# Attention and expert stages of a spiking layer with routed experts: two steps of the expert weights' split set a block apart, scatters ahead of attention, first expert rows loaded inside it, sums moved to GpSimd

## The reference, cut to what matters

```python
xn = layernorm(x)                                   # x: 2 x 2048 x 256, float32
x + attn(xn) + ffn(xn)

# attn, D = 256, 16 heads of 16
Q, K, V = [spike(layer_norm(xn @ W.T + b, g, beta) - 1) for each of q, k, v]    # 0 or 1
attn = Dh - (q_sum + k_sum - 2 Q K^T) + log_pe_bias                            # no softmax
out = spike(attn * scale @ V - 0.5)
out = spike(layer_norm(out @ Wo.T + bo, go, betao) - 1)

# ffn, E = 8 experts, top 2
scores, idx = top_k(softmax(xn @ router_w.T), 2); scores /= sum(scores)
out = sum over the two experts of score * (silu(xn @ up[:, :256]) * (xn @ up[:, 256:])) @ down
```

## Time and profile before

| what | us |
| --- | --- |
| median of 3 runs (lowest to highest) | 446.23 (444.5 to 446.79) |
| the profiled execution's own time | 447.23 |
| its span, first to last instruction | 445.4 |
| TensorE busy in it | 369.1 (83%) |
| VectorE, ScalarE, GpSimd busy | 272.4, 226.1, 231.5 |
| mean granted TensorE clock | 0.951 of full |

### The profile page before, as it was taken

The page is one execution under the profiler, slowest core; times in us unless marked ns, Lnnn a source line. Parts: engine busy times, 40 slices in busy tenths (PEclk is TensorE's granted clock), DMA queues, the critical chain, the costliest instruction groups (busy, mean ns, idle before and its releaser), DMA issues.

```text
span 445.4 us, 9584 instructions
## 1 busy us (share of the span) xinstructions
PE 369.1 (83%) x2421; PEld 297.8 (67%) x2430; DVE 272.4 (61%) x899; ACT 226.1 (51%) x716; POOL 231.5 (52%) x203
## 2 busy tenths in 40 slices
PE   4399848899888987666945999999999999999980
PEld 1233738888888554444744888888888888888760
DVE  5699799987877425555735455555555555555530
ACT  1456773777876543333422455555555555555530
POOL 3646424777773025543713455547374656554663
PEclk9589896999999999999979899999999999999995
DMA  8842031344544025655454455646475566564653
GB/s 262 283 166 72 0 93 51 121 133 154 173 140 147 1 60 167 192 189 165 146 164 143 66 96 96 104 83 107 82 113 93 100 97 101 93 105 85 104 60 35
DMA packets 43399, 51.71 MB, mean 116 GB/s; under 512 B 6278, under 2 KB 37000, under 8 KB 43368
## 3 DMA queue, kind: packets, MB, share of 16 engines
q0 software_dynamic: 13888, 19.30, 24.2%
q1 hardware_dynamic: 27488, 30.21, 23.9%
q10 hardware_dynamic: 1992, 1.85, 1.3%
HBM read 27.86 MB, written 23.48 MB: 115 GB/s over the span
## 4 chain that ended last, share of the span: by engine, by line
PE 50%; DVE 17%; issue 11%; POOL 8%; ACT 6%; DMA 5%; SPq 1%; POOLq 0%; DVEq 0%; ACTq 0%
PE bank L1129 14%; PE bank L1131 13%; PE bank L1130 13%; POOL rstd L702 3%; PE bank L1253 3%; DMA xn<-x 3%; POOL slot_x L684 3%; PE bank L1271 3%; DVE xn L802 2%; ACT junk L487 2%; DMA ex<-slot_x 2%; DVE xst L780 2%; DVE qk_spk L1000 2%; DVE exT_l L969 2%; ACT gact L532 1%
## 5 line engine op out<-in xcount | busy, mean ns | idle before, releaser
L731 POOL DMA_INDIRECT out<-ey,dest x71 | 109.5, 1542 | 88.9 <-DMA out<-ey,dest 35.6
L1031 DVE TENSOR_TENSOR hid<-gact,bank 128x256 f32<-128x256 f32 x71 | 29.8, 420 | 77.9 <-ACT gact L532 77.9
L684 POOL DMA_INDIRECT slot_x<-xn,pos x64 | 63.2, 987 | 26.0 <-issue 22.8
L1129 PE MATMUL bank<-ew,exT_h 128*128 x142 | 63.1, 444 | 5.4 <-DVE exT_l L969 5.4
L1129 PE MATMUL bank<-w_h,xT_h 128*128 128x256 f32 x192 | 57.8, 301 | 1.2 <-DVE xT_l L810 0.9
L1130 PE MATMUL bank<-ew,exT_h 128*128 x142 | 57.0, 401 | 0.0
L532 ACT ACTIVATE gact<-bank 128x256 f32<-128x256 f32 x71 | 27.2, 383 | 58.1 <-PE bank L1131 58.1
L1131 PE MATMUL bank<-ew,exT_l 128*128 x142 | 56.7, 399 | 0.0
L1130 PE MATMUL bank<-w_l,xT_h 128*128 128x256 f32 x192 | 55.1, 287 | 0.0
L1131 PE MATMUL bank<-w_h,xT_l 128*128 128x256 f32 x192 | 55.0, 286 | 0.0
L487 ACT ACTIVATE junk<-bank 128x256 bf16<-128x256 f32 x96 | 35.9, 380 | 27.5 <-PE bank L1131 27.2
(11 more groups left out here) (202 smaller groups left out, 901.9 us busy)
## 6 DMA issues: line engine op xcount, KB each, us to landing
ex<-slot_x SPq DMA_DIRECT2D x71, 130.0 KB, 2.5
ew_f<-experts SPq DMA_DIRECT2D x24, 256.0 KB, 3.2
xo<-x SPq DMA_DIRECT2D x16, 256.0 KB, 3.1
out<-xo SPq DMA_DIRECT2D x16, 256.0 KB, 2.3
xn<-x SPq DMA_DIRECT2D x6, 512.0 KB, 12.2
out<-ey,dest POOLq DMA_INDIRECT x71, 3.8
xn<-x SPq DMA_DIRECT2D x4, 256.0 KB, 3.7
w_f<-w_all ACTq DMA_DIRECT2D x1, 1024.0 KB, 7.5
```

Of the source, the lines that this page charges most:

```text
L684: pool.indirect_dma_start(slot_x, bass.IndirectOffsetOnAxis(ap=pos[:, k, t:t + 1], axis=0), xn[:, t, :], None).then_inc(s[done], 16)
L731: pool.indirect_dma_start(out, bass.IndirectOffsetOnAxis(ap=dest[:, j:j + 1], axis=0), ey[:, j % 4, :], None, compute_op=ALU.add).then_inc ...
L1031: v.tensor_tensor(hid[:, m % 2, :], gact[:, m % 2, :], h_ps[m % 2][:, F:2 * F], ALU.mult).then_inc(s["hid_done"], 1)
L1129: mm(dst, a_h, b_h, start=first, stop=False)
```

## The change

- `ATTENTION_PIECES` now says piece 14+k in block k. ScalarE takes the high part in that block, VectorE the low part one block later; SP loads the piece in the block of that number, as before.
- All 32 tiles and the 7 pads are scattered before GpSimd's first step of attention.
- GpSimd adds x for blocks 0 to 13 (`add_block`), VectorE for 14 and 15 alone.
- `ex` no longer lies over `ew_f`, but behind `exT_l`. Its first four tiles are loaded at block 9 instead of 14, no longer after the last piece. Tiles 4 to 7 are loaded between the last four stores instead of behind them. `row_places` of tiles 0 to 3 goes from the start of the expert stage into VectorE's blocks 12 to 15.
- `landed` has one count per tile: 16 where nothing is waited for, else the round's; the other three follow by adding 16 in a register. The rows of zeros are stored in eight DMAs of 64 rows instead of four of 128, so that `y_out` starts from 32.

```diff
-SCATTERED = 26
-ATTENTION_PIECES = {1 + k: POOL_PIECES + 6 + k for k in range(PIECES - POOL_PIECES - 6)}
-FIRST_ROWS = 14
+ATTENTION_PIECES = {k: POOL_PIECES + 6 + k for k in range(PIECES - POOL_PIECES - 6)}
+FIRST_ROWS = 9
+POOL_SUMS = NB - 2
...
-        ex = place_in(r_e)("ex", [P, 4, ROW])
...
         exT_l = put("exT_l", [P, 2, KC, P], F32R)
+        ex = put("ex", [P, 4, ROW])
...
             def store_block(a):
-                sp.wait_ge(s["spk_added"], a + 1)
+                if a < POOL_SUMS:
+                    sp.wait_ge(s["pool_added"], a + 1)
+                else:
+                    sp.wait_ge(s["spk_added"], a - POOL_SUMS + 1)
...
-                if a + 1 in ATTENTION_PIECES:
-                    load_late(ATTENTION_PIECES[a + 1])
+                if a in ATTENTION_PIECES:
+                    load_late(ATTENTION_PIECES[a])
                 if a >= 3:
                     store_block(a - 3)
                 if a == FIRST_ROWS:
+                    sp.wait_ge(s["half_summed"], 1)
                     sp.wait_ge(s["scattered"], 16 * TOPK * (NT - FREED_MORE))
                     sp.wait_ge(s["pads_done"], 16 * PC)
-                    sp.wait_ge(s["piece_l"], PIECES - POOL_PIECES)
                     for j in range(4):
                         load_tile(j, j)
-            for a in range(NB - 3, NB):
-                store_block(a)
-            for j in range(4, 8):
-                load_tile(j, j % 4)
+            load_tile(4, 0)
+            load_tile(5, 1)
+            store_block(NB - 3)
+            load_tile(6, 2)
+            store_block(NB - 2)
+            load_tile(7, 3)
+            store_block(NB - 1)
...
-            for t in range(SCATTERED):
-                pool.wait_ge(s["proj_done"], G3 * (t + LEAD))
+            for t in range(NT):
+                pool.wait_ge(s["proj_done"], G3 * min(t + LEAD, NT - 2))
                 scatter(t)
+            pool.wait_ge(s["pads_placed"], 1)
+            pool.wait_ge(s["pads_marked"], 32)
+            for c in range(PC):
+                scatter_pad(c)
...
+            def add_block(a):
+                pool.wait_ge(x_back[a % 4], 16 * (a // 4 + 1))
+                pool.wait_ge(s["w_spk"], B * (a + 1))
+                both = xo[:, a % 4, :, :]
+                g.tensor_tensor(both, both, spk(a), ALU.add).then_inc(s["pool_added"], 1)
...
             for a in range(NB):
                 out_rstd(a)
-                if a < NT - SCATTERED:
-                    scatter(SCATTERED + a)
...
+                if 1 <= a <= POOL_SUMS:
+                    add_block(a - 1)
...
-                pool.dma_start(out[B * N + u * P:B * N + (u + 1) * P, :], pad_row[:, 0:D]).then_inc(y_out[u], 16)
+                for half in range(2):
+                    rows = B * N + u * P + half * (P // 2)
+                    pool.dma_start(out[rows:rows + P // 2, :], pad_row[0:P // 2, 0:D]).then_inc(y_out[u], 16)
...
-                    landed[0:1, j:j + n, :].rearrange("p j r -> p (j r)"), engines=[mybir.EngineType.Pool],
+                    landed[0:1, j:j + n], engines=[mybir.EngineType.Pool],
                     min_val=16, max_val=16 * (SLOT_TILES // 4 + 2))
+                for u in range(1, n):
+                    pool.reg_add(later[u], pool.to_reg(counts[u]), 16)
...
-                for r in range(4):
-                    pool.wait_ge(y_out[r], counts[r])
+                for r in range(j % 4, 4):
+                    pool.wait_ge(y_out[r], count)
+                for r in range(j % 4):
+                    pool.wait_ge(y_out[r], count_later)
...
                 if a >= 2:
                     out_variance(a - 2)
-                if a >= 3:
-                    add_x(a - 3)
-                if a in ATTENTION_PIECES:
-                    piece_lower(ATTENTION_PIECES[a], ATTENTION_PIECES[a])
+                if a - 1 in ATTENTION_PIECES:
+                    piece_lower(ATTENTION_PIECES[a - 1], ATTENTION_PIECES[a - 1])
                 if a >= 2:
                     spike_out(a - 2)
+                if a >= NB - 4:
+                    row_places(a - (NB - 4), a - (NB - 4), 1)
```

More of the change, by code:

```diff
@@ L106, in spiking_moe @@
         half_gate = keep("half_gate", [P, 4])
-        landed = keep("landed", [P, SLOT_TILES, 4], I32)
+        landed = keep("landed", [P, SLOT_TILES], I32)
         pad_row = keep("pad_row", [P, ROW])
@@ L181, in spiking_moe @@
         first_f = put("first_f", [P, SLOT_TILES])
-        landed_w = put("landed_w", [P, SLOT_TILES, 4], I32)
-        assert (SLOT_TILES * 5 + 32) * 4 <= 3 * E * NT * 4
+        assert SLOT_TILES <= 3 * E * NT
         r_a = max(ends[r_q], ends[r_v])
@@ L189, in spiking_moe @@
         w_l = put("w_l", [P, KC, G3 * D], F32R)
-        r_e = r_a + 2 * KC * G3 * D * 4
         ew_f = put("ew_f", [P, 2, PW])
-        ex = place_in(r_e)("ex", [P, 4, ROW])
-        assert ends[r_e] >= ends[r_a]
         put = place_in(r_a)
@@ L199, in spiking_moe @@
         ey = put("ey", [P, 4, D])
-        r_b = ends[r_e]
+        r_b = ends[r_a]
         put = place_in(r_b)
@@ L244, in spiking_moe @@
             dve_order pool_order w_gone
-            s_done o_done o_turned oT_set out_proj w_ssq w_var w_rstd w_spk spk_added scattered_first scattered_more gate_half gate_set landed_set""".split()
+            s_done o_done o_turned oT_set out_proj w_ssq w_var w_rstd w_spk pool_added spk_added scattered_first scattered_more gate_half gate_set landed_set""".split()
         names.append("eps_set")
@@ L380, in _ @@
             for r in range(4):
-                sp.wait_ge(y_out[r], 16 + 16 * len(range(r, SLOT_TILES, 4)))
+                sp.wait_ge(y_out[r], 32 + 16 * len(range(r, SLOT_TILES, 4)))
         @block.scalar
@@ L717, in _ @@
             pool.wait_ge(s["landed_set"], 1)
+            later = [pool.alloc_register(f"later{u}") for u in range(4)]
             def landings_before(j, n):
                 _, counts = nc.values_load_multi_w_load_instructions(
-                    landed[0:1, j:j + n, :].rearrange("p j r -> p (j r)"), engines=[mybir.EngineType.Pool],
+                    landed[0:1, j:j + n], engines=[mybir.EngineType.Pool],
                     min_val=16, max_val=16 * (SLOT_TILES // 4 + 2))
+                for u in range(1, n):
+                    pool.reg_add(later[u], pool.to_reg(counts[u]), 16)
@@ L724, in landings_before, with send @@
                 return counts
-            def send(j, counts):
+            def send(j, count, count_later):
                 pool.wait_ge(s["dest_done"], j + 1)
                 pool.wait_ge(s["ey_done"], j + 1)
-                for r in range(4):
-                    pool.wait_ge(y_out[r], counts[r])
+                for r in range(j % 4, 4):
+                    pool.wait_ge(y_out[r], count)
+                for r in range(j % 4):
+                    pool.wait_ge(y_out[r], count_later)
                 pool.indirect_dma_start(out, bass.IndirectOffsetOnAxis(ap=dest[:, j:j + 1], axis=0),
@@ L739, in _ @@
                     counts = landings_before(j, n)
-                send(j, counts[j % 4 * 4:j % 4 * 4 + 4])
+                send(j, counts[j % 4], later[j % 4])
         @block.vector
@@ L842, in _ @@
             consts = []
-            for width in (E, E * NT, SLOT_TILES, PC, NT):
+            for width in (E, E * NT, SLOT_TILES, PC, NT, SLOT_TILES):
                 consts.append(rc[:, at:at + width])
                 at += width
-            rev, keep_run, tile_start, pad_no, y_place = consts
+            rev, keep_run, tile_start, pad_no, y_place, rounds = consts
             step(v.tensor_copy(xn[:, :, D], y_place))
@@ L960, in landings @@
                 settled()
-                for r in range(4):
-                    step(v.tensor_scalar(landed_w[:, :, r], first_f[:, :], float(P * (7 - r)), None, ALU.add))
+                step(v.tensor_tensor(first_f[:, :], first_f[:, :], tile_start, ALU.is_equal))
                 settled()
-                v.tensor_scalar(landed[:, :, :], landed_w[:, :, :], 9, 4, ALU.logical_shift_right,
-                                ALU.logical_shift_left).then_inc(s["landed_set"], 1)
+                step(v.tensor_tensor(first_f[:, :], first_f[:, :], rounds, ALU.mult))
+                settled()
+                v.tensor_scalar(landed[:, :], first_f[:, :], 16.0, None, ALU.add).then_inc(s["landed_set"], 1)
             def keep_exl(j, m):
@@ L1053, in expert @@
                     keep_exl(j + 2, m + 2)
-                row_places(j, m, i + 1)
+                if not early(j, 4):
+                    row_places(j, m, i + 1)
                 if not early(j, 1):
@@ L1101, in _ @@
             out_variance(NB - 2)
-            add_x(NB - 3)
             spike_out(NB - 2)
@@ L1441 @@
         first_token[None, :] + no[:, None],
+        np.broadcast_to(16 * (np.arange(SLOT_TILES) // 4 + 1), (P, SLOT_TILES)),
     ], axis=1).astype(np.float32)
```

8 lines of the change are left out of this document (1 added, 7 removed).

## The result

The changed kernel takes **422.87 us** (median of 4 runs, 421.56 to 423.13) against 446.29 for the kernel before beside it: a ratio of 0.948, 95% interval [0.944, 0.951]. Predicted were 418.4 us, range 412 to 430. Its profiled execution took 423.13 us, with a span of 421.3: 24.1 us less than before.

A forecast was written before the change was run, and what follows sets the result against it. TensorE was taken as bound, waiting in attention on a 5.38 us ring through VectorE's spikes and ScalarE's copy, plus two expert-row holes. Span 445.4 - 25.7 - 2.1 = 417.6, execution 419.4, about 418.4 us against the median; range 412 to 430.

The forecast's parts named there:

- the forecast's own case: Whole kernel: the time falls between 412 and 425 us, chance 0.76.
- rival 1: Attention: a new three-block ring replaces the old, 4.4 to 4.9 us a block, 426 to 430 us; chance 0.17.
- The split: Attention: subtracting the block before's copy cuts the 5.38 us ring; floor 3.62 us a block, gain at most 14.3 us.
- Rival 2: Attention: the ring was not the bound or is not cut; blocks stay at 5.4 us, 432.5 us; chance 0.04.
- Scatters and pads first: Before attention: 24.5 us of work fills GpSimd's idle hole; first power stays at 163.5, block 3's turn at 166.3.
- The sum on GpSimd: Attention: each sum takes 1.45 us (ends 1.35 and 2.05); GpSimd's block 2.8 us, under TensorE's 3.62.
- Rival 3: Attention: slower, as GpSimd's sum passes TensorE's pace; gains gone at 4.3 us, about 456 at 5; chance 0.03.
- What is late next: Attention: three-block ring through sum, store and loads, 3.7 us a block; eleven blocks 39.7 + 1.0 us, gain 14.1.
- The pair port: Attention: GpSimd's sums and VectorE's two-input subtractions exclude each other but miss each other; put at nothing.
- Rows in time: Attention's end: the 5.61 us hole goes; last turn but one to first up-projection 5.7 us against 10.81, gain 5.1.
- The second hole: Expert stage: the 4.67 us wait before tile 4 goes; first to fifth up-projection 10.6 us against 17.10, gain 6.5.
- GpSimd's counts: Kernel's end: fewer count loads let the last send start at 435.2 instead of 437.30, gain 2.1; hidden in the loop.

The follow-up runs named there:

- e1_piece_first: The changed kernel with SP starting the load of a piece ahead of its wait for the stored block: 418.70 us, ratio 0.938.
- e2_x_last: The changed kernel with SP's order per block piece, store, then the wait for the stored block and the x load: 417.82 us, ratio 0.932.
- e12_x_last_counts_of_before: e2_x_last with GpSimd's counts and the four stores of zeros as before the change: 454.83 us, ratio 0.978.
- e5: The changed kernel with all sums back on VectorE: 421.28 us, ratio 0.942.
- e8: The kernel before with the split's shift as its only edit: 435.64 us, ratio 0.976.
- e9: e2_x_last with the fourteen sums back on VectorE: 454.75 us, ratio 0.978.
- The last four kernels: e2_x_last with sums on VectorE, e2_x_last repeated, the changed kernel with old counts, e2_x_last with old counts: 454.75, 452.68, 462.63, 454.83 us.

## Why the prediction was right or wrong

**The time** came out 4.5 us above the forecast and inside the range. Of the 4.5 us, 3.7 are in the span; the rest is that the profiled execution lay 1.0 us above the median before and 0.3 after. The measured time falls into the forecast's own case, 412 to 425, and still the mechanism has something of rival 1: a new ring did take the place of the old. The prediction named the sign of it (the copy waits for the piece's DMA) but the wrong ring. That the size stayed under rival 1's 426 to 430 is in part luck: the ring through SyncE was priced nowhere.

**The split**: right. The ring of 5.38 us was the bound, and the shift cuts it: undone it costs 10.0 us in the blocks (64.1 against 54.1), alone it brings 11.2 (53.2 against 64.4), and the floor is reachable (47.5 us in e1_piece_first and e2_x_last). Rival 2 is out.

**Scatters and pads first**: right. First power at 163.47 (163.5 forecast), the last pad right ahead of it, the turn of block 3 at 165.86 (166.3). The scatters took 1.26 us each as put, the pads 1.26 for most and not 1.34. But the late first power cost TensorE nothing, where the text counted two us as lost: from the turn of block 0 to that of block 3 it is 9.22 us here and 9.25 with the shift alone, whose first power starts at 160.9.

**The sum on GpSimd**: the size was off, without effect. 1.18 us in place of 1.45, and the power beside it 0.71 to 0.74 in place of 1.09 in most blocks (its median fell to 0.71). Rival 3 was far away: even with 2.4 us of sum the ratio stayed at 0.948, though some of it reached the blocks. In the prediction's ring the sum stands with 1.55 us and in its own paragraph with 1.45, and rival 3's 456 should be 457 to 458 by its own prices; neither matters for the forecast.

**What is late next** is the step that failed. It put a ring over three blocks, through the sum, of 3.7 us a block, and 1 us for ten blocks. The runs show that the sum is in no ring at its length of 1.18 us. The text had the store, its landing, the load of x and the piece as links of that long chain, but did not see that these close a ring by themselves: the next store stands right behind the piece in the same queue. By my own prices that ring would have been 2.3 + 0.4 + 0.5 = 3.2 us and harmless. But 2.3 is the landing in the old order and pace; right behind two loads of 256 KB it was 3.5, and once 5.2. That makes 4.4 us a block, where the prediction's sign of being right was 3.6 to 3.8. In us: the forecast gave the eleven blocks 40.7; TensorE alone needs 38.3 (e2_x_last; the last blocks are shorter than 3.61, which I had left out), and SP's ring added 6.6 to that, 1.7 of them by the one late landing, for 44.9. So the errors are 1.4 too much for the 39.7 and 5.6 too little for the 1.0.

**The pair port**: rightly put at nothing for this change. VectorE's nine subtractions of the stretch took 0.686 to 0.693 us, its 128x2 operations 0.16 to 0.17: none was caught. In the kernel with late scatters two were held. The 128x2 operation ends with GpSimd's sum (191.14 and 191.10). The subtraction began 0.6 us ahead of the sum, while GpSimd was in a scatter, and ended 0.55 us behind it, nearly its own length; what held it before the sum began is not shown. The Trainium skill (SBUF — State Buffer, the section SBUF: two separate sides) calls this an exclusive lock for the whole instruction, for VectorE operations with two SBUF inputs or in a two-port mode. The ends agree with it; the 128x2 operation has a single input, and no run shows in which mode it ran. Even caught, an operation need not cost: in e2_x_last one subtraction took 1.38 us and one 1.01, and the blocks kept TensorE's pace.

**Rows in time**: right. 5.51 us from the last turn but one to the first up-projection (5.7), with 1.24 us of waiting for the low part of tile 0, as named. The clock stayed full through it, and through a wait of 2.70 us in attention. Four DMA starts in block 9 took 1.94 us and delayed nothing on the path.

**The second hole**: right in kind, 0.9 us short. 11.46 instead of 10.6: 0.95 at the first down-projection as said, the rest in the waits for low parts. Rows late again costs 12.2 us from the last turn but one to the fifth up-projection, against the 10.9 us that the change gained there and 11.6 forecast.

**GpSimd's counts**: the end brought 1.6 of 2.1 us, as the gap ahead of the third-last send is 0.96 us with the wait for a landing, and the last send still waits its 1.84 us behind the one before. The term that was put at nothing, the stretch from the fifth tile to the last rows, brought 1.2: "in the loop this is hidden behind TensorE" is not quite so ahead of the first sends. The first send comes 2.2 us sooner behind the start of the stores of zeros (11.1 us before the change, 9.0 after), and with the old counts ScalarE sometimes waits for landings behind it (0.8 us before the change, 3.3 in e12_x_last_counts_of_before). That this made the 1.2 is not shown: the kernel with the shift alone has the old counts and 184.1 us in that stretch, as the changed kernel has.

The sum of it: +3.7 (blocks, with their start), -0.2, +0.9, -1.2, +0.5 is 3.7 us, the difference of the spans 421.3 and 417.6.

## What to carry to other kernels

When a ring is cut, write out the in-order queues next to it turn by turn: for each wait, in which turn was the thing it waits for started? Four buffers are no slack if the queue starts a store one turn before it waits for it; move the wait behind everything else that the queue can start. And price a transfer by what runs ahead of it in its queue, not by its median in another order. Here the order in SyncE's queue was worth more than the sums on GpSimd, which gained nothing measurable with the ring or without it.

## What the runs showed of the hardware that I had not expected

- A store of 256 KB landed in 2.2 us (median) when it was started ahead of the load of x and, where there was one, 1.6 us or more behind the piece (e2_x_last), and in 3.4 us when it was started behind both, in the same queue, with the same bytes in all (the changed kernel). With the load of x alone 0.4 us ahead of it and the piece behind it, it was 3.2 (e1_piece_first).
- GpSimd's power on 128x2 has a median of 1.07 to 1.09 us in the four kernels in which VectorE sums (before, e5, e8, e9) and of 0.71 to 0.72 in those in which GpSimd does. With VectorE's sum, that operation starts 0.16 to 0.19 us ahead of the power in each block. From the last turn but one to the first up-projection it is 5.51 us with the sums on GpSimd and 5.90 with them on VectorE (e5, e9), a gain which I had not counted.
- A VectorE operation of 0.15 us on 128x2 took 1.45 us beside one sum on GpSimd. On the path a small operation would have cost as much there as a large one.
- GpSimd's sum with one float32 and one bfloat16 operand took 1.17 us, less than its subtraction of the same shape with two float32 operands, 1.32 on average here (1.35 in the earlier trace rows).
- The last four kernels had a projection stage 31 to 39 us longer with the same instructions, while the kernel before took 19 us more beside them. The order of e2_x_last had a ratio of 0.973 there instead of 0.932. Why the two kernels lost unequally is not shown.
